# Alternating small TensorE products between output partitions in a fused image network

## The reference

```python
x = x + mamba(ln(x))           # two Mamba-2 blocks, a scan over 1024 tokens
t = t + experts0(ln(t))        # 8 experts, two hidden layers, softmax gate
x = x + logsum(ln(x), acc1)    # log of a product of exp(x) with accumulators
t = t + experts1(ln(t))        # 8 experts, top 2, gelu
x = x + logsum(ln(x), acc2)
t = t + lstm(ln(t))            # an LSTM along each image row
x = x + conv_attention(ln(x))  # 7 x 7 depthwise convolution, then attention
t = t + experts3(ln(t))        # 8 experts, top 2, gelu
```

## Time and profile before

| | |
|---|---|
| median of 3 runs | 3164.37 us (3163.59 to 3166.41) |
| profiled execution, first to last instruction | 3157.1 us |
| mean granted TensorE clock of the profiled execution | 0.822 of full speed |
| TensorE matmuls busy | 2771.7 us, 88% |
| TensorE weight loads busy | 2231.2 us, 71% |
| VectorE busy | 1953.5 us, 62% |
| ScalarE busy | 1668.0 us, 53% |
| GpSimd busy | 874.9 us, 28% |

### The profile page before, as it was taken

How to read it: one execution, slowest core, us unless ns; L and a number is a source line. 1 busy time by engine, 2 the same in 40 slices (tenths; PEclk the granted TensorE clock), 3 DMA queues, 4 the chain that set the end, 5 groups by cost and what they waited for, 6 DMA issues and landing times. The chain is left out here.

```text
span 3157.1 us, 64810 instructions
## 1 busy us (share of the span) xinstructions
PE 2771.7 (88%) x22240; PEld 2231.2 (71%) x22240; DVE 1953.5 (62%) x8535; ACT 1668.0 (53%) x5755; POOL 874.9 (28%) x1499
## 2 busy tenths in 40 slices
PE   4477888899999999999999999999998787887667
PEld 3366666678888788888888888788777564555556
DVE  5466666676667677777766667677754324555454
ACT  1245555566666666666665666666654423443333
POOL 2233222233233333323333333333311000000444
PEclk8677766688888888888888888888886688998888
DMA  2000000000000100000000000000000001000000
GB/s 100 14 17 18 18 19 19 19 19 19 21 21 20 32 19 19 19 19 19 19 19 19 21 21 25 27 19 19 19 17 9 3 2 28 1 1 1 8 10 11
DMA packets 54039, 59.12 MB, mean 19 GB/s; under 512 B 26576, under 2 KB 45136, under 8 KB 53328
## 3 DMA queue, kind: packets, MB, share of 16 engines
q1 hardware_dynamic: 53712, 54.99, 6.0%
HBM read 42.37 MB, written 4.19 MB: 15 GB/s over the span
## 5 line engine op out<-in xcount | busy, mean ns | idle before, releaser
L1072 DVE TENSOR_TENSOR_SCAN r_c<-r_wk 64x24 f32<-64x24 f32 x1024 | 244.3, 239 | 490.4 <-ACT r_wk L1058 486.5
L1058 ACT ACTIVATE r_wk<-psL 64x16 f32<-64x16 f32 x1024 | 189.1, 185 | 678.1 <-PE psL L1048 659.9
L1152 PE MATMUL psL<-img,dg 128*128 128x128 f32 x2646 | 452.7, 314 | 0.0
L1047 PEld LDWEIGHTS psL<-r_h,lv 128*64 128x64 f32 x2048 | 235.6, 162 | 291.1 <-DVE r_h L1077 162.9
L1047 PE MATMUL psL<-r_h,lv 128*64 128x8 f32 x2048 | 324.6, 231 | 80.6 <-DVE r_h L1077 74.8
L1152 PEld LDWEIGHTS psL<-img,dg 128*128 128x128 f32 x2646 | 378.4, 215 | 11.8 <-issue 3.9
L1049 PE MATMUL psL<-r_h,lv 128*64 128x8 f32 x2048 | 326.4, 232 | 0.0
L1048 PE MATMUL psL<-r_h,lv 128*64 128x8 f32 x2048 | 304.7, 222 | 0.0
L1077 DVE SCALAR_TENSOR_TENSOR r_h<-r_wk,r_tc 64x8 f32<-64x8 f32 x1024 | 196.3, 192 | 115.0 <-ACT r_tc L1063 101.5
L1063 ACT ACTIVATE r_tc<-r_c 64x8 f32<-64x8 f32 x1024 | 215.5, 210 | 83.8 <-DVE r_c L1072 37.7
L1048 PEld LDWEIGHTS psL<-r_h,lv 128*64 128x64 f32 x2048 | 252.7, 171 | 0.0
(11 more groups left out here) (376 smaller groups left out, 6558.8 us busy)
## 6 DMA issues: line engine op xcount, KB each, us to landing
accb<-acc_in SPq DMA_DIRECT2D x64, 512.0 KB, 4.3
a_xy<-a_E SPq DMA_DIRECT2D x512, 16.0 KB, 1.8
W<-pack_in SPq DMA_DIRECT2D x1, 3165.0 KB, 13.7
x6d<-X SPq DMA_DIRECT2D x64, 32.0 KB
out_x<-X SPq DMA_DIRECT2D x32, 64.0 KB, 1.6
X<-x_in SPq DMA_DIRECT2D x1, 1856.0 KB, 17.7
W<-pack_in SPq DMA_DIRECT2D x1, 1331.0 KB, 5.8
X<-x_in SPq DMA_DIRECT2D x1, 192.0 KB
```

The costliest lines, as they stand in the source:

```text
L1047: nc.tensor.matmul(psL[0:64, par, c:c + LB], lv[:, 0], h, start=False, stop=False, skip_group_check=True)
L1058: nc.scalar.activation(o, psL[0:64, par, c:c + 2 * LB].rearrange("p (g b) -> p g b", b=LB), ACT.Tanh).then_inc(sem("r_gi"), 1)
L1072: v.tensor_tensor_scan(r_c3[:, t % 2, :], r_wk[:, 0:24], r_wk[:, 30:54], 0.0, ALU.mult, ALU.add).then_inc(sem("r_c"), 1)
L1152: last = nc.tensor.matmul(o, dg[:, ky * KT + kx], rows[:, :, ky, kx:kx + IMG], start=(n == 0), stop=(n == KT * KT - 1))
```

## The change

Three layers write the output partitions of neighbouring products alternately; a fourth edit concerns the state product's place.

- State space Y: the loop over heads `h` becomes the outer one and the image halves `j` the inner one, so that partitions 0 to 31 and 32 to 63 alternate. The number of yields is the same.
- Log-sum layers: product `t` writes partitions 0 to 63 when it is even and 64 to 127 when it is odd. The result then stands in 128 partitions with half as many columns. VectorE's reciprocal has the shape 128x16 in place of 64x32, and its scaling becomes two instructions of 64x128 elements.
- Second expert layer: each product with 128 weight columns becomes two with 64, into partitions 0 to 63 and 64 to 127.
- State product: its two products are issued together behind two yields.

```diff
-            for j in range(J):
-                yield
+            yield
+            yield
+            for j in range(J):
                 last = nc.tensor.matmul(bk[64 * j:64 * j + 64, 256:256 + P], u["bc"][:, 0, j].rearrange("p b n -> p (b n)"),
                                         u["xy"][:, j], start=True, stop=True)
...
-            for j in range(J):
-                if j:
+            for h in range(NH):
+                if h:
                     yield
-                for h in range(NH):
-                    if h and h % 2 == 0:
-                        yield
+                for j in range(J):
                     last = nc.tensor.matmul(bk[TT * j:TT * j + TT].rearrange("p (b h d) -> p h b d", b=B4, h=NH)[:, h], u["RM"][:, j * NH + h],
                                             u["xw"][:, j, h], start=True, stop=True)
...
-                last = nc.tensor.matmul(ps[0:64, 0, 0:288].rearrange("p (h b t) -> p h b t", h=2, t=16)[:, :, :, t],
+                half = slice(64 * (t % 2), 64 * (t % 2) + 64)
+                last = nc.tensor.matmul(ps[half, 0, 0:144].rearrange("p (h b u) -> p h b u", h=2, u=8)[:, :, :, t // 2],
                                         accb[k][:, t], c_eT[k][:, :, :, t], start=True, stop=True)
...
-            v.tensor_tensor(c_q[k][:].rearrange("p b (h t) -> p h b t", h=2), pv[:, :, 0:B], bc(c_r[k][:], 2, B), ALU.mult)\
-                .then_inc(sem(c + "_q"), 1)
+            for odd in (0, 1):
+                half = slice(64 * odd, 64 * odd + 64)
+                last = v.tensor_tensor(c_q[k][:].rearrange("p b (h u o) -> p h b u o", h=2, o=2)[:, :, :, :, odd], pv[half, :, 0:B],
+                                       bc(c_r[k][half], 2, B), ALU.mult)
+            last.then_inc(sem(c + "_q"), 1)
...
-                    last = nc.tensor.matmul(psC[:, j, e * C:(e + 1) * C], u["h"][:, e, j * P:(j + 1) * P], w("m1w2", e * C, (e + 1) * C),
-                                            start=False, stop=(e == E - 1))
+                    for half in range(2):
+                        r = slice(64 * half, 64 * half + 64)
+                        last = nc.tensor.matmul(psC[r, j, e * C:(e + 1) * C], u["h"][:, e, j * P + 64 * half:j * P + 64 * half + 64],
+                                                w("m1w2", e * C, (e + 1) * C), start=False, stop=(e == E - 1))
```

More of the change, by code:

```diff
@@ L289, in build @@
         c_eT = [sb(f"c_eT{k}", P, 2, B + 1, 16) for k in (0, 1)]
-        c_r = [sb(f"c_r{k}", 64, J, 16) for k in (0, 1)]
+        c_r = [sb(f"c_r{k}", P, J, 8) for k in (0, 1)]
         c_q = [sb(f"c_q{k}", 64, B, TT) for k in (0, 1)]
@@ L869, in prod_dve @@
             dve.wait_ge(sem(c + "_mm"), i1)
-            pv = ps[0:64, 0, 0:288].rearrange("p (h b t) -> p h b t", h=2, b=B + 1)
+            pv = ps[:, 0, 0:144].rearrange("p (h b u) -> p h b u", h=2, b=B + 1)
             st.did(v.reciprocal(c_r[k][:], pv[:, :, B]))
```

## The result

The changed kernel takes 3079.64 us (median of 4 runs, 3071.16 to 3081.93). The kernel before took 3163.98 on the same chip (4 runs, 3155.33 to 3166.41). The ratio is 0.973, with a 95% interval of 0.971 to 0.975. The forecast was 3080. The sum came out where it should, but its terms did not: the full turns gave less than forecast and the five early turns more.

What follows compares the result with a forecast made beforehand. TensorE was taken to bound the loop where it comes later than `r_h`; 3.2 us a turn over 22 turns (71), 8 for early turns and 5 for first and last make 84: 3164.4 to 3080 us, range 3040 to 3135.

Steps and rivals of the forecast that it cites:

- Y, 1.34 us a turn: State space Y: alternating takes 6 pitches of 0.057 from each of four pieces, 0.34 us each, 1.34 a turn.
- The second expert layer, 1.3 us: Second expert layer: 32 passes become 32 pairs at pitch 0.057, saving 1.7 us, less 0.4 for weight-width changes.
- 0.66 of it in step 13 (0.83 late): Expert saving in step 13: 0.66 us, taken to fit since TensorE's LSTM product started 0.83 after `r_h` was ready.
- The log-sum layers, 0.6 us: Log-sum layers, steps 22 to 28: shorter products less VectorE's split scaling, net 0.6 us a turn.
- The 0.44 of step 24: Log-sum products, eight half-clock passes before 1310.15: four pitches of 0.11 go, 0.44 of 0.53 us available.
- I count half, 8: Five early turns, without convolution and with more idle PE: half the full-turn saving each, 8 us together.
- the term that it could not sum: TensorE's clock, low for 16 us at the turn's end: 3 us more or less a turn means 33 us in all.
- Half the gain: Rival, chance 0.20: expert pairs run at 0.11 and width changes remain, 1.54 us a turn, 3124 us.
- its second form: Same rival, 3124 us: ScalarE and VectorE work carries over, making `r_h` later by half of what PE saves.
- The clock fell a second time: Rival, chance 0.07: a second low-clock stretch in each full turn makes it slower; two such stretches, 3243 us.
- It does nothing: Rival, chance 0.05: TensorE already takes the other half's products from its queue, `r_h` hides the rest, 3160 us.
- Not side by side: Rival, chance 0.05: the halves' loads and matmuls follow one another; no gain, 0.5 us a turn lost, 3175 us.

Runs made afterwards that it cites:

- the later pair: Whole change, plus last four half products of image half 0 and VectorE's scaling of their result one step later: 3064.34 us, 0.970 of the kernel before.

## Why the prediction came out as it did

**Y, 1.34 us a turn.** Right: alone it took 0.33 + 0.35 + 0.33 + 0.33 = 1.34 out of its four steps. The pitch of 0.057 and the six pitches a piece held.

**The second expert layer, 1.3 us.** The pitch of a pair was right (0.058 for 0.057) and the time was not. The layer took 0.13 + 0.11 + 0.24 from steps 13, 15 and 16 and gave 0.11 back in step 17: 0.37. The step that failed is "0.66 of it in step 13 (0.83 late)". The prediction compared the saving with the lateness of `r_h` alone and forgot a nearer wait. Products on `m_h` can be no earlier than ScalarE's last activation, and the 0.38 of that wait took most of it, as the later pair shows. In steps 15 and 16 the prediction's own rule gives 16 x 0.052 - 0.2 = 0.63, where 0.35 came. There the sum itself was wrong. It took a pitch for every pass, but n passes have n - 1 pitches from first to last start, and its piece of 12 is two, of 4 and 8, with convolution taps between. The kernel before in step 16, same view as the earlier trace rows:

```profile
1292.99 0.55 PE L944 MATMUL psC<-W,m_h 128*128 128x64 f32 x4
...
1293.88 1.00 PE L944 MATMUL psC<-W,m_h 128*128 128x64 f32 x8
```

With 0.27 for a single one these take 0.28 + 0.73 = 1.01. In the changed kernel the same pieces take 0.45 - 0.22 = 0.23 (the 8 passes of L949 before L1157 last 0.45) and 0.69 - 0.22 = 0.47, together 0.70. So the passes of step 16 gave 0.31 and not 12 x 0.052 = 0.62. By the same count the piece in step 13 was worth 1.63 - 0.93 = 0.70 (15 pitches of 0.109, then 16 pairs of 0.058) and not 16 x 0.052 = 0.83, before the wait.

In step 17 the 0.11 was lost because the earlier TensorE meets VectorE's `state`, which comes behind the scaling of L949's own result. VectorE's timeline of the changed kernel in step 17:

```profile
1319.30 0.69 DVE L1004 TENSOR_TENSOR m_big<-psC,m_cw 128x512 f32<-128x512 f32 x1 [0.94 <-PE psC L949]
...
1320.34 0.27 DVE L627 TENSOR_TENSOR state<-a_sd,psA 128x128 f32<-128x128 f32 x1
1320.54 0.82 DVE L1082 SCALAR_TENSOR_TENSOR r_h<-r_wk,r_tc 64x8 f32<-64x8 f32 x1
```

L1004 waits for the products, `state` stands behind it, and Y waits 0.23 for `state`. At the end of this step `r_h` is done at 1320.54 + 0.82 = 1321.36 and L1052 starts at 1321.44: the room is used up. This cause is read from the rows, not tested.

**The log-sum layers, 0.6 us.** Alone they gave 0.18 + 0.44 + 0.08 in steps 23, 24 and 27 and cost 0.04 + 0.19 in steps 26 and 28: 0.47. Step 23 had been counted at nothing. The 0.44 of step 24 came exactly, but the reason given for it, four shorter pitches, is not needed: it is enough that the products stand in the other half than the next LSTM product. Step 28 was mis-sized: two scalings have 288 ns each where 270 was taken, but the prediction put TensorE's transpose behind them and not `r_h`, which is queued behind both, so the 0.2 from shorter products fell away too.

**The sum.** 1.34 + 0.37 + 0.47 = 2.18 a turn, and 72.72 - 70.55 = 2.17 was measured, where 3.2 was forecast. In 22 turns that is 47.5 instead of 71.

**The early turns.** "I count half, 8" failed the other way: 28.2. Turns of the early five in the kernel before (first fence) and in the changed one (second), columns as above:

```profile
434.30:512.70 78.40, 68.72 (x517) 54.17 (x516) 50.64 (x241) 45.56 (x167) 23.59 (x43) 0.70 0.07 19
```

```profile
424.50:497.20 72.70, 60.46 (x547) 46.01 (x546) 51.01 (x242) 45.52 (x167) 23.35 (x43) 0.71 0.07 20
497.20:573.00 75.80, 63.86 (x547) 48.23 (x546) 50.88 (x242) 45.62 (x167) 23.36 (x43) 0.68 0.07 20
573.00:642.40 69.40, 56.75 (x548) 43.09 (x547) 50.70 (x242) 45.33 (x167) 23.39 (x43) 0.77 0.07 22
```

Three equal turns of the changed kernel differ by 6.4 us, in the order of their clock. Over the five the granted clock rose from 0.70 to 0.73, so the share of time at half clock, twice what is missing to 1, fell from 0.60 to 0.54: 389.8 x 0.60 - 361.6 x 0.54 = 39 us less at half clock, worth half of that where TensorE sets the pace. So an estimated 19 of the 28.2 is the clock, and 9, or 1.8 a turn, the same work as in the full turns. Where the clock stayed up can be read: in the profiled execution of the kernel before it fell a second time amid four of the five early turns, as in the earlier trace rows, in that of the changed kernel amid two. The last early turn of the changed kernel has one long stretch at full clock there:

```profile
582.90:620.50 37.60, 32.36 (x357) 24.71 (x357) 30.84 (x136) 28.15 (x95) 16.13 (x24) 1.00 0.01 2
```

Why the clock did not fall, the runs do not tell. In the kernel before all five turns stand at 0.70; in every other kernel here they differ. The prediction had named the clock as the term that it could not sum and put it into the range, but thought of the full turns, where it stayed at 0.85.

**The rivals.** "Half the gain" was partly true in its second form: of the 1.06 a turn that was missing in the full turns, waits for other engines took about half (0.38 for `m_h`, 0.11 for `state`), the wrong count of pitches most of the rest. The clock fell a second time in none of the 22 full turns. "It does nothing" is refuted by the time, though its premise, that TensorE looks ahead in its queue, held. "Not side by side" is refuted, with the rule behind it: the Trainium skill's page "TensorE: Matmul & The Clock Gate", Part 3, lets a load overlap matmuls in flight only where the row group differs, and here pairs of one row group go at 0.058. A change of weight width does cost: from L944 to L949 it is 1310.15 - 1309.84 = 0.31 in the changed kernel. In the kernel before, where L944 was the product and L941 the bias, both 128 wide, it was 1284.64 - 1284.41 = 0.23, by the earlier trace rows and this row of the same view:

```profile
1284.41 0.39 PE L941 MATMUL psC<-bias,ones 65*128 65x512 bf16 x1
```

That the forecast met the median within 1 us is luck: 23.5 us too much for the full turns and 3.7 for the first and last ones (5 forecast, 1.3 measured) stand against 20.2 too little for the early ones, and the remaining 7 us lie between the profiled pair (77) and the medians (84).

## What to carry to other kernels

Before you count a saving on the bounding engine, list every wait of the shortened work itself, its own inputs first, and not only the loop's main dependency. Put products of few output partitions into another part of the array than the latency-critical product that follows them: here that alone gave what alternation gave in steps 23 and 24. The order within a short stretch mattered less, since the queue was searched over at least four passes. After such a change look at the second engine's queue: an instruction split in two in front of the critical one gives back what the first engine won.

## What was not expected of the hardware

- TensorE starts matmuls ahead of their order when the other half of its columns is free: L1051 at 1325.69 before L822 products that stand ahead of it, and pairs of L946 over a distance of four passes. The same page and part of the Trainium skill says that matmuls start and end strictly in order; this trace differs.
- VectorE's small instructions stretch to the end of a large GpSimd one. The changed kernel's GpSimd and VectorE in steps 17 and 13:

```profile
1320.08 1.26 POOL L793 TENSOR_TENSOR m_big<-m_big 128x512 f32<-128x512 f32 x1 [1.60 <-DVE m_big L1004]
```

```profile
1310.16 1.10 DVE L1077 TENSOR_TENSOR_SCAN r_c<-r_wk 64x24 f32<-64x24 f32 x1 [0.31 <-ACT r_wk L1063]
```

The first ends at 1321.34, and the `r_h` of step 17 above, 0.82 instead of some 0.15, at 1321.36. The second is one of 52 L1077 of over 0.6 us, against a median of 0.20; they and 57 such L1082 end 0.02 to 0.06 behind an instruction of GpSimd. The Trainium skill's page "SBUF — State Buffer", section "SBUF: two separate sides", tells of a port that VectorE and GpSimd lock against each other; the trace agrees. In step 17 this sets the time of `r_h`.
